# Feed-forward of a decoder kernel: quantisation over all 704 columns at once, input quantised by quarters

## The chip, the cores and the metric

The kernel runs on one core of a Trainium2 chip, as one program. The metric is the device time of one execution in microseconds (us), here the median of three runs. The core has five engines that run their own instruction streams and meet at semaphores: TensorE (PE in the profile; PEld is its weight load), VectorE (DVE), ScalarE (ACT), GpSimd (POOL) and SyncE (SP), which issues the transfers.

## The reference

Four batches of 1024 rows with 256 columns pass through two layers: a state-space scan, a cross attention and a feed-forward in the first, a cosine attention, an alignment and a mixture of experts in the second. Each adds to the residual stream x. The change lies in the first layer's feed-forward alone:

```python
BLOCK = 16
_GRID = [0.0, 0.5, 1.0, 1.5, 2.0, 3.0, 4.0, 6.0]
_MID = [0.25, 0.75, 1.25, 1.75, 2.5, 3.5, 5.0]

def fp4_quant_dequant(x):
    xb = x.reshape(shape[:-1] + (shape[-1] // BLOCK, BLOCK))
    scale = jnp.maximum(jnp.max(jnp.abs(xb), axis=-1, keepdims=True) / 6.0, 1e-12)
    xn = xb / scale
    idx = jnp.searchsorted(_MID, jnp.abs(xn))
    return (_GRID[idx] * jnp.sign(xn) * scale).reshape(shape)

def fp4_linear(x, w):
    return jnp.einsum('bsk,nk->bsn', fp4_quant_dequant(x), fp4_quant_dequant(w))

gate, y = fp4_linear(x, w_gate), fp4_linear(x, w_up)     # 256 -> 704
h = jax.nn.silu(gate) * y
out = fp4_linear(h, w_down)                              # 704 -> 256
x = x + L0_ffn(_layernorm(x))
```

So the normalised input is quantised in blocks of 16 columns, multiplied with two weight matrices of 704 columns, combined to a hidden row of 704 columns, quantised again and multiplied back to 256 columns.

## The kernel before, in words

One batch is worked off at a time, in 8 tiles of 128 rows. Each engine has its own function for the stage, with the order of its work written out by hand; semaphores carry the rest. The stage runs four times in an execution, once per batch.

`quantize` (L2177) does ten VectorE steps on a list of pieces: largest absolute value per block (L2187), scaling of it (L2189), reciprocal (L2190), scaling (L2191), multiplication of the row (L2192), two steps that find the power of two of each element (L2194, L2196), two rounding steps (L2198, L2199), and the multiplication back (L2210). For each step it goes through all pieces, and each instruction waits on VectorE's own semaphore for the step before of its own piece. With two pieces, two independent chains alternate.

`quantize_z` (L715) does this for the normalised input `z`; a piece is a pair of tiles, 512 columns. Pairs 0 and 1 are quantised one at a time within the cross attention before. Pairs 2 and 3 come together at the head of `ffn_dve` (L1000), as two pieces.

VectorE then does, for each tile k, `hidden(k)`: the product of silu(gate) and up out of PSUM (L1007), then `quantize` of the hidden row as two pieces of 352 columns (L1010), then, for the tile before the last one begun, `add`: the down result to x (L1017) with the statistics for the next normalisation. `hidden(k + 1)` stands ahead of `add(k - 1)`.

TensorE does for each tile `gate_up` (8 float32 matmuls, L938, 16 records in the trace; waits until the product of the tile before has been read), `turn` (6 transposes of the quantised hidden row, L947; waits for both pieces at L943) and `down` (6 matmuls, L956). In the loop `gate_up(k + 1)` comes first, then `turn(k)`, then `down(k - 1)`. The transposes of the input (`transpose_z`, L269) stand ahead of that loop: pair 0, gate_up(0), then pairs 1, 2 and 3 in PSUM banks 5, 6 and 7, each waiting for its pair of quantised input. `turn` uses banks 4 and 5, `down` bank 6.

ScalarE copies the transposed input to `zT` (`keep_zT`, L275), computes silu (L982) and copies the transposed hidden row (L995 to L997).

Of the kernel before, what the change touches and what calls it, by code (L numbers as in the profile page):

```python
# [29 lines left out]
FF = 704  # L30
FQ = FF // 2
FK = [(k * P, min(P, FF - k * P)) for k in range((FF + P - 1) // P)]
QB = 16
# [52 lines left out]
def program(nc, t, out):  # L86

    ctx = ExitStack()
    with ctx:
# [122 lines left out]
        def tile_stats(v, own, src, k, n, to=by_stage):  # L212

            own.wait()
            own(v.bn_stats(to.stat[:, k, :], src))
            if k >= 1:
                aggregate(v, own, k - 1, n, to)
            if k == NT - 1:
                own.wait()
                aggregate(v, own, k, n, to)  # L220
# [42 lines left out]
        def transpose_z(pe, j, wait_tile, pairs=range(NT // 2), first_bank=0):  # L263
            for g in pairs:
                for k in (2 * g, 2 * g + 1):
                    wait_tile(k)
                    for c in range(DC):
                        q = (k % 2) * DC + c
                        last = pe.transpose(psum[:, first_bank + g, q * P:(q + 1) * P], z[:, k, c * P:(c + 1) * P], ident[:, :])  # L269
                last.then_inc(zT_psum, 1)  # L270

        def keep_zT(a, j, pairs=range(NT // 2), first_bank=0):
            for g in pairs:
                a.wait_ge(zT_psum, 4 * j + g + 1)
                a.activation(zT[:, :, 2 * g * P:(2 * g + 2) * P].rearrange("p c (k x) -> p k c x", k=2),  # L275
                             psum[:, first_bank + g, :].rearrange("p (k c x) -> p k c x", k=2, c=DC),
                             ACT.Copy).then_inc(zT_ready, 1)


        r = Region(arena)  # L280
# [15 lines left out]
        r = Region(arena, scan_end)  # L296
# [400 lines left out]
        r = Region(arena, scan_end)  # L697
# [17 lines left out]
        def quantize_z(v, own, pairs):  # L715

            n = 2 * D
            quantize(v, own, [(z[:, 2 * h:2 * h + 2, :].rearrange("p k d -> p (k d)"),
                               z_scaled[:, n * h:n * (h + 1)], z_power[:, n * h:n * (h + 1)],
                               f_amax[:, n * h // QB:n * (h + 1) // QB], f_inv[:, n * h // QB:n * (h + 1) // QB])  # L720
                              for h in pairs],
                     lambda piece, last: own.bring(last, zq_ready, pairs[0] + piece + 1))
# [199 lines left out]
        r = Region(arena, scan_end)  # L922
        silu_gate = r.take(2, FF)
        hid = r.take(2, FF)
        h_scaled, h_power = r.take(FF), r.take(FF)
        hT = r.take(2, len(FK), P)
        h_amax, h_inv = r.take(2, FQ // QB), r.take(2, FQ // QB)
        assert r.at <= zq.at - 2 * NT * (D + D // QB)

        def ffn_pe(pe, own, j):  # L930

            def gate_up(k):
                if k >= 1:
                    pe.wait_ge(hid_made, k)
                for i, wT in enumerate((gateT, upT)):
                    for half in range(2):
                        for c in range(DC):
                            last = pe.matmul(psum[:, 2 * i + half, 0:FQ], zT[:, c, k * P:(k + 1) * P],  # L938
                                             wT[:, c, half * FQ:(half + 1) * FQ], start=c == 0, stop=c == DC - 1)
                last.then_inc(gu_psum, 1)  # L940

            def turn(k):
                pe.wait_ge(h_ready, 2 * (k + 1))  # L943
                if k >= 1:
                    pe.wait_ge(hT_ready, 3 * k)
                for i, (at, wide) in enumerate(FK):
                    last = pe.transpose(psum[0:wide, 4 + i // 4, (i % 4) * P:(i % 4 + 1) * P],  # L947
                                        hid[:, k % 2, at:at + wide], ident[:, :])
                last.then_inc(ht_psum, 1)

            def down(k):
                pe.wait_ge(hT_ready, 3 * (k + 1))
                if k >= 1:
                    pe.wait_ge(fres_done, k)
                for i, (_, wide) in enumerate(FK):
                    last = pe.matmul(psum[:, 6, 0:D], hT[0:wide, k % 2, i, :], downT[0:wide, i, :],  # L956
                                     start=i == 0, stop=i == len(FK) - 1)
                last.then_inc(down_psum, 1)

            pe.wait_ge(ffn_w_in, 16 * 3)  # L960
            transpose_z(pe, j, lambda k: pe.wait_ge(zq_ready, k // 2 + 1), pairs=(0,), first_bank=4)
            pe.wait_ge(zT_ready, 4 * j + 1)
            gate_up(0)
            transpose_z(pe, j, lambda k: pe.wait_ge(zq_ready, k // 2 + 1), pairs=(1, 2, 3), first_bank=4)
            for k in range(NT):
                if k + 1 < NT:
                    if k % 2:
                        pe.wait_ge(zT_ready, 4 * j + (k + 1) // 2 + 1)
                    gate_up(k + 1)
                if k == 0:  # L970
                    pe.wait_ge(zT_ready, 4 * j + 2)
                turn(k)
                if k >= 1:
                    down(k - 1)
            down(NT - 1)

        def ffn_act(a, own, j):
            def silu(k):
                a.wait_ge(gu_psum, k + 1)
                if k >= 2:  # L980
                    a.wait_ge(hid_made, k - 1)
                a.activation(silu_gate[:, k % 2, :].rearrange("p (a x) -> p a x", a=2),  # L982
                             psum[:, 0:2, 0:FQ], ACT.Silu).then_inc(sg_ready, 1)

            keep_zT(a, j, pairs=(0,), first_bank=4)
            silu(0)
            keep_zT(a, j, pairs=(1, 2, 3), first_bank=4)
            for k in range(NT):
                if k + 1 < NT:
                    silu(k + 1)  # L990
                q = k % 2
                a.wait_ge(ht_psum, k + 1)
                if k >= 2:
                    a.wait_ge(down_psum, k - 1)
                a.activation(hT[:, q, 0:4, :].rearrange("p k x -> p (k x)"), psum[:, 4, :], ACT.Copy).then_inc(hT_ready, 1)  # L995
                a.activation(hT[:, q, 4, :], psum[:, 5, 0:P], ACT.Copy).then_inc(hT_ready, 1)
                a.activation(hT[0:64, q, 5, :], psum[0:64, 5, P:2 * P], ACT.Copy).then_inc(hT_ready, 1)  # L997

        def ffn_dve(v, own, b, next_n, next_j):
            quantize_z(v, own, (2, 3))  # L1000

            def hidden(k):
                q = k % 2
                v.wait_ge(sg_ready, k + 1)
                if k >= 2:
                    v.wait_ge(ht_psum, k - 1)
                own.bring(v.tensor_tensor(hid[:, q, :].rearrange("p (a x) -> p a x", a=2),  # L1007
                                          silu_gate[:, q, :].rearrange("p (a x) -> p a x", a=2),
                                          psum[:, 2:4, 0:FQ], ALU.mult), hid_made, k + 1)
                quantize(v, own, [(hid[:, q, i * FQ:(i + 1) * FQ], h_scaled[:, i * FQ:(i + 1) * FQ],  # L1010
                                   h_power[:, i * FQ:(i + 1) * FQ], h_amax[:, i], h_inv[:, i]) for i in range(2)],
                         lambda piece, last: own.bring(last, h_ready, 2 * k + piece + 1))

            def add(k):
                v.wait_ge(down_psum, k + 1)
                xk = x_all[:, b * NT + k, :]
                own.bring(v.tensor_tensor(xk, xk, psum[:, 6, 0:D], ALU.add), fres_done, k + 1)  # L1017
                tile_stats(v, own, xk, k, next_n)

            hidden(0)  # L1020
            for k in range(NT):
                if k + 1 < NT:
                    hidden(k + 1)
                if k >= 1:
                    add(k - 1)
            norm_x(v, own, b, next_n, next_j, tiles=range(NT // 2))
            add(NT - 1)
# [6 lines left out]
        r = Region(arena, after_parts)  # L1034
# [139 lines left out]
        r = Region(arena, scan_end)  # L1174
# [37 lines left out]
        r = Region(arena)  # L1212
# [257 lines left out]
        r = Region(arena, WAVES * LW)  # L1470
# [16 lines left out]
        r = Region(arena, beside_dtw)  # L1487
# [725 lines left out]
        r = Region(arena)  # L2213
# [446 lines left out]
```

## Time and profile before

| | us |
|---|---|
| median of three runs | 3328.77 (3325.11 to 3330.94) |
| the profiled execution | 3329.13 |
| its span, first to last instruction | 3327.4 |
| TensorE busy in the span | 2758.6 (83%) |
| VectorE busy | 2433.5 (73%) |
| ScalarE busy | 1339.7 (40%) |
| GpSimd busy | 622.2 (19%) |
| mean granted TensorE clock | 0.906 of full speed |

In the chain that ended last, TensorE holds 59% and VectorE 25% of the span. The four feed-forward stages lie at about 427 to 513, 941 to 1026, 1453 to 1538 and 1931 to 2016 us. The table is an average over all stages; what a change of the feed-forward is worth is read from these four stretches. Rows of a timeline give the start, the duration, engine, line, operation, output and input, and the count of instructions that were merged; in square brackets stands the idle time of the engine just before and what ended it.

### The profile page before, as it was taken

The page shows a single profiled execution, that of the slowest core. Times are in us where ns is not written, and L with a number is a line of the kernel's source. Part 1 is how long each engine was busy: PE and PEld are TensorE (multiplying, and loading weights), DVE is VectorE, ACT ScalarE, POOL GpSimd, SP SyncE. Part 2 cuts the span into 40 slices and gives each one's busy share as a digit, 9 for nine tenths or more (in the row PEclk, how much of TensorE's full clock was granted, in tenths as well). Part 3 has the DMA queues.
Part 4 walks back from the last instruction along what each step waited for, and adds up shares of the span by engine and source line. Part 5 has one row for each costly group of instructions (what it writes and reads, how often), then busy time and mean ns, then how long its engine had stood idle before and what let it go on. Part 6 is the DMA issues. An engine that isn't in the chain of part 4 may idle for free.

```text
span 3327.4 us, 36552 instructions
## 1 busy us (share of the span) xinstructions
PE 2758.6 (83%) x12264; PEld 1576.6 (47%) x12264; DVE 2433.5 (73%) x4936; ACT 1339.7 (40%) x2455; POOL 622.2 (19%) x426
## 2 busy tenths in 40 slices
PE   4226888997889997889998888992369999999998
PEld 2003764444665344665345764441135656566564
DVE  6996687997687997678998586006877676776766
ACT  2323326773425773424773325553640131411313
POOL 2444000332100333100233000001000040310404
PEclk9557899998989998989998989996669999999999
DMA  5001000001000001000001000006020000000000
GB/s 159 0 0 45 1 1 7 23 20 53 1 1 5 22 20 57 1 1 1 23 23 46 10 0 7 23 20 127 0 34 1 1 14 1 1 14 1 14 1 13
DMA packets 57635, 65.93 MB, mean 20 GB/s; under 512 B 27757, under 2 KB 46690, under 8 KB 56802
## 3 DMA queue, kind: packets, MB, share of 16 engines
q1 hardware_dynamic: 57441, 63.51, 7.1%
q8 instruction: 103, 1.69, 0.2%
q14 instruction: 91, 0.74, 0.1%
HBM read 45.22 MB, written 9.88 MB: 17 GB/s over the span
## 4 chain that ended last, share of the span: by engine, by line
PE 59%; DVE 25%; issue 5%; ACT 4%; POOL 2%; DMA 1%; SPq 0%; DVEq 0%; ACTq 0%; POOLq 0%
PE psum L1712 14%; PE psum L383 8%; DVE arena L543 6%; PE psum L938 4%; PE psum L1772 3%; PE psum L790 3%; PE psum L1052 3%; DVE arena L538 3%; PE psum L956 3%; PE psum L770 2%; PE psum L373 2%; PE psum L374 2%; PE psum L269 2%; PE psum L781 2%; PE psum L1071 1%
## 5 line engine op out<-in xcount | busy, mean ns | idle before, releaser
L1712 PE MATMUL psum<-weights,arena 128*128 128x384 f16 x3072 | 534.9, 329 | 5.1 <-DVE arena L2068 4.0
L383 PE MATMUL psum<-arena,weights 128*128 128x512 f32 (+1 forms) x1024 | 522.6, 593 | 5.0 <-ACT arena L457 5.0
L2071 DVE SCALAR_TENSOR_TENSOR arena<-psum,arena 128x384 f32<-128x384 f32 x480 | 295.7, 616 | 193.7 <-PE psum L1712 182.6
L457 ACT ACTIVATE arena<-psum,minus_scale 128x512 f32<-128x512 f32 x512 | 350.7, 686 | 215.1 <-PE psum L383 213.3
L1712 PEld LDWEIGHTS psum<-weights,arena 128*128 128x128 f16 x3072 | 304.2, 99 | 194.3 <-issue 8.8
L598 POOL TENSOR_TENSOR arena<-arena 128x1024 f32<-128x1024 f32 x128 | 274.0, 2141 | 598.6 <-DVE arena L543 598.0
L543 DVE TENSOR_TENSOR_SCAN arena<-weights,arena 128x1026 f32<-128x1026 f32 x128 | 293.9, 2296 | 18.4 <-ACT weights L450 3.8
L246 POOL TENSOR_SCALAR shifted<-mean_var 128x4 f32<-128x4 f32 x40 | 9.8, 245 | 1287.1 <-DVE mean_var L223 1287.1
L1947 POOL TENSOR_TENSOR arena<-arena 128x512 f32<-128x512 f32 x112 | 147.6, 1321 | 509.8 <-ACT arena L1886 499.2
L383 PEld LDWEIGHTS psum<-arena,weights 128*128 128x128 f32 (+1 forms) x1024 | 166.1, 163 | 98.7 <-ACT arena L457 12.1
L450 ACT ACTIVATE weights<-arena,weights 128x512 f32<-128x512 f32 x256 | 169.1, 712 | 102.8 <-DVE arena L543 102.8
L373 PE MATMUL psum<-arena 128*128 128x512 f16 x512 | 194.5, 380 | 4.7 <-DMA arena<-arena 4.7
L374 PE MATMUL psum<-arena 128*128 128x512 f16 x512 | 194.2, 379 | 0.0
L1772 PE MATMUL psum<-weights,arena 128*128 128x512 f16 x768 | 172.5, 379 | 7.8 <-DVE x_all L2100 4.6
L938 PE MATMUL psum<-weights,z_both 128*128 128x352 f32 x512 | 171.0, 490 | 6.6 <-DVE arena L1007 3.9
L275 ACT ACTIVATE z_both<-psum 128x512 f32<-128x512 f32 x96 | 55.3, 594 | 262.1 <-PE psum L269 262.0
L551 DVE TENSOR_TENSOR arena<-arena,psum 128x1024 f32<-128x1024 f32 x128 | 156.3, 1221 | 4.4
L2100 DVE SCALAR_TENSOR_TENSOR x_all<-psum,arena,x_all 128x256 f32<-128x256 f32 x256 | 122.3, 483 | 50.0 <-PE psum L1772 44.9
L538 DVE TENSOR_TENSOR arena<-arena,psum 128x1024 f32<-128x1024 f32 x128 | 154.8, 1209 | 3.8 <-PE psum L356 3.6
L269 PE MATMUL psum<-ident,z_both 128*128 128x128 f32 x384 | 72.9, 351 | 101.7 <-DVE z_both L260 80.1
L356 PE MATMUL psum<-arena,weights 96*128 96x512 bf16 x128 | 55.8, 436 | 104.8 <-DVE arena L551 96.2
L1886 ACT ACTIVATE arena<-psum,arena 128x256 f32<-128x256 f32 x256 | 107.5, 471 | 87.5 <-PE psum L1772 87.3
(324 smaller groups left out, 4867.0 us busy)
## 6 DMA issues: line engine op xcount, KB each, us to landing
arena<-arena SPq DMA_DIRECT2D x64, 128.0 KB, 2.3
arena<-head_inv SPq DMA_DIRECT2D x32, 256.0 KB, 3.4
weights<-in_qkv SPq DMA_DIRECT2D x2, 3072.0 KB, 17.1
weights<-gate_upT_kept SPq DMA_DIRECT2D x4, 1408.0 KB, 6.4
x_all<-in_x SPq DMA_DIRECT2D x4, 1024.0 KB, 11.9
weights<-in_cWkv SPq DMA_DIRECT2D x4, 1024.0 KB, 11.3
out<-x_all SPq DMA_DIRECT2D x4, 1024.0 KB, 4.4
weights<-downT_kept SPq DMA_DIRECT2D x4, 640.0 KB, 7.0
```

Of the source, the lines that this page charges most:

```text
L373: pe.matmul(psum[:, i % 3, :], keys, q_parts[:, hd, at], start=True, stop=False)
L374: pe.matmul(psum[:, i % 3, :], keys, q_swapped_parts[:, hd % 2, at], start=False, stop=True).then_inc(s2_psum, 1)
L383: pe.matmul(psum[0:rows, 3 + turn % 2, :], value_and_ones(kt, hd), expd[:, i % 2, :], start=kt == 0, stop=kt == NT - 1).then_inc(pv2_done, 1)
L450: a.activation(dA[:, j % RING, m, 1:], dt[:, m, half * HALF:(half + 1) * HALF], ACT.Exp, scale=a_neg[:, m, s:s + 1]).then_inc(da_ready, 1)
L457: a.activation(expd[:, i % 2, :], psum[:, i % 3, :], ACT.Exp, bias=minus_scale[:, :], scale=SCALE / QK ** 2).then_inc(exp_done, 1)
L538: v.tensor_tensor(to[:, :, 1:], u[:, :, at], both(5 + 2 * j % 3), ALU.mult).then_inc(w_done, 1)
L543: v.tensor_tensor_scan(flat, dA[:, j % RING].rearrange("p m x -> p (m x)"), flat, 0.0, ALU.mult, ALU.add).then_inc(scan_done, 1)
L598: g.tensor_tensor(y[:, :, at], y[:, :, at], h[:, j % RING, :, 1:], ALU.add).then_inc(y_added, 1)
L938: last = pe.matmul(psum[:, 2 * i + half, 0:FQ], zT[:, c, k * P:(k + 1) * P], wT[:, c, half * FQ:(half + 1) * FQ], start=c == 0, stop=c == ...
L1712: last = pe.matmul(psum[:, n % PROJ_BANKS, 0:W3], zT_parts[:, of_z, c, k * P:(k + 1) * P], w_parts[:, c, e, of_w, :], start=c == 0 and j == 0,
L1772: last = pe.matmul(psum[:, O_BANKS[u % 4], :], ao_parts[:, of_a, k * P:(k + 1) * P], o_parts[:, m, of_w, :], start=j == 0, stop=j == 2)
L2071: step_ = v.scalar_tensor_tensor(qkv[:, k, :], src, router_w[:, k, e:e + 1], qkv[:, k, :], ALU.mult, ALU.add)
```

## The change

The hidden row is quantised as one piece of 704 columns instead of two of 352, in one chain of ten instructions; TensorE waits for one count per tile instead of two. Of the input, pair 2 alone is quantised at the head of the stage, and pair 3 after `hidden(1)`, ahead of `hidden(2)`. TensorE's transposes of pair 2 go to bank 7, and those of pair 3 to bank 7 as well, after `turn(1)` and `down(0)`, when the copy of pair 2 is done. ScalarE's copy of pair 3 moves to the same place in its order.

```diff
-        h_amax, h_inv = r.take(2, FQ // QB), r.take(2, FQ // QB)
+        h_amax, h_inv = r.take(FF // QB), r.take(FF // QB)
...
             def turn(k):
-                pe.wait_ge(h_ready, 2 * (k + 1))
+                pe.wait_ge(h_ready, k + 1)
...
             gate_up(0)
-            transpose_z(pe, j, lambda k: pe.wait_ge(zq_ready, k // 2 + 1), pairs=(1, 2, 3), first_bank=4)
+            transpose_z(pe, j, lambda k: pe.wait_ge(zq_ready, k // 2 + 1), pairs=(1,), first_bank=4)
+            transpose_z(pe, j, lambda k: pe.wait_ge(zq_ready, k // 2 + 1), pairs=(2,), first_bank=5)
             for k in range(NT):
...
                 turn(k)
                 if k >= 1:
                     down(k - 1)
+                if k == 1:
+                    pe.wait_ge(zT_ready, 4 * j + 3)
+                    transpose_z(pe, j, lambda t: pe.wait_ge(zq_ready, t // 2 + 1), pairs=(3,), first_bank=4)
             down(NT - 1)

         def ffn_act(a, own, j):
...
             silu(0)
-            keep_zT(a, j, pairs=(1, 2, 3), first_bank=4)
+            keep_zT(a, j, pairs=(1,), first_bank=4)
+            keep_zT(a, j, pairs=(2,), first_bank=5)
...
                 a.activation(hT[0:64, q, 5, :], psum[0:64, 5, P:2 * P], ACT.Copy).then_inc(hT_ready, 1)
+                if k == 1:
+                    keep_zT(a, j, pairs=(3,), first_bank=4)

         def ffn_dve(v, own, b, next_n, next_j):
-            quantize_z(v, own, (2, 3))
+            quantize_z(v, own, (2,))
...
-                quantize(v, own, [(hid[:, q, i * FQ:(i + 1) * FQ], h_scaled[:, i * FQ:(i + 1) * FQ],
-                                   h_power[:, i * FQ:(i + 1) * FQ], h_amax[:, i], h_inv[:, i]) for i in range(2)],
-                         lambda piece, last: own.bring(last, h_ready, 2 * k + piece + 1))
+                quantize(v, own, [(hid[:, q, :], h_scaled, h_power, h_amax, h_inv)],
+                         lambda piece, last: own.bring(last, h_ready, k + 1))
...
             for k in range(NT):
                 if k + 1 < NT:
                     hidden(k + 1)
+                if k == 0:
+                    quantize_z(v, own, (3,))
                 if k >= 1:
                     add(k - 1)
```

## Rows read from the trace of the kernel before

**Rows 1.** Stretches: busy time by engine (count), granted clock, DMA share, GB/s.

```profile
core 0: us, PE busy (x) PEld busy (x) DVE busy (x) ACT busy (x) POOL busy (x), PEclk, DMA share, GB/s
431.00:437.00 6.00, 1.25 (x7) 0.69 (x5) 6.00 (x15) 1.25 (x2) 0.00 (x0) 1.00 0.00 0
469.50:478.00 8.50, 8.50 (x38) 5.89 (x37) 8.05 (x25) 1.63 (x5) 0.00 (x0) 1.00 0.01 2
502.00:506.00 4.00, 3.35 (x11) 2.96 (x12) 1.44 (x5) 0.92 (x3) 0.00 (x0) 0.50 0.00 0
...
954.00:957.00 3.00, 3.00 (x8) 1.81 (x8) 3.00 (x13) 0.00 (x0) 0.00 (x0) 0.70 0.00 0
```

**Rows 2.** Timeline of the first feed-forward's steady part, all engines.

```profile
472.90 5.00 PE L938 MATMUL psum<-weights,z_both 128*128 128x352 f32 x16
...
477.40 0.41 DVE L1017 TENSOR_TENSOR x_all<-x_all,psum 128x256 f32 x1
...
477.74 0.82 PE L947 MATMUL psum<-ident,arena 128*128 128x128 f32 x6
...
478.73 0.89 DVE L1007 TENSOR_TENSOR arena<-arena,psum 128x704 f32<-128x704 f32 x1 [0.38 <-ACT arena L982]
...
481.27 5.00 PE L938 MATMUL psum<-weights,z_both 128*128 128x352 f32 x16
```

**Rows 3.** Timeline of VectorE: product and quantising of tile 1, two pieces.

```profile
445.39 0.89 DVE L1007 TENSOR_TENSOR arena<-arena,psum 128x704 f32<-128x704 f32 x1 [0.64 <-ACT arena L982]
446.31 0.94 DVE L2187 TENSOR_REDUCE arena<-arena 128x22 f32<-128x352 f32 x2
...
451.56 0.95 DVE L2210 TENSOR_TENSOR arena<-arena 128x352 f32<-128x352 f32 x2
452.43 0.88 DVE L1007 TENSOR_TENSOR arena<-arena,psum 128x704 f32<-128x704 f32 x1
```

**Rows 4.** Timeline of VectorE: input pair 1, one piece, in the cross attention.

```profile
413.77 0.69 DVE L2187 TENSOR_REDUCE arena<-z_both 128x32 f32<-128x512 f32 x1
414.49 0.18 DVE L2189 TENSOR_SCALAR arena<-arena 128x32 f32<-128x32 f32 x1
414.71 0.35 DVE L2190 RECIPROCAL arena<-arena 128x32 f32<-128x32 f32 x1
...
415.31 0.69 DVE L2192 TENSOR_TENSOR arena<-z_both,arena 128x512 f32<-128x512 f32 x1
416.04 0.43 DVE L2194 TENSOR_SCALAR arena<-arena 128x512 int32<-128x512 int32 x1
...
418.42 0.69 DVE L2210 TENSOR_TENSOR z_both<-arena 128x512 f32<-128x512 f32 x1
419.03 0.41 DVE L905 TENSOR_TENSOR x_all<-x_all,psum 128x256 f32 x1
```

**Rows 5.** Timeline of VectorE: input pairs 2 and 3, and what follows.

```profile
429.39 1.28 DVE L2187 TENSOR_REDUCE arena<-z_both 128x32 f32<-128x512 f32 x2
...
437.64 0.88 DVE L1007 TENSOR_TENSOR arena<-arena,psum 128x704 f32<-128x704 f32 x1
```

**Rows 6.** Groups of VectorE by line and form, 0 to 45 us (weights' quantising).

```profile
L2198 DVE SCALAR_TENSOR_TENSOR arena<-arena 128x1408 f32<-128x1408 f32 x3 | 4.7, 1610 | 0.0
...
L2194 DVE TENSOR_SCALAR arena<-arena 128x1408 int32<-128x1408 int32 x3 | 2.5, 880 | 0.0
...
L2190 DVE RECIPROCAL arena<-arena 128x88 f32<-128x88 f32 x3 | 1.8, 657 | 0.0
```

**Rows 7.** Timeline of the second feed-forward's start, all engines.

```profile
943.79 1.28 DVE L2187 TENSOR_REDUCE arena<-z_both 128x32 f32<-128x512 f32 x2
...
951.58 1.55 PE L269 MATMUL psum<-ident,z_both 128*128 128x128 f32 x8 [2.79 <-DVE z_both L2210]
...
952.98 6.39 PE L938 MATMUL psum<-weights,z_both 128*128 128x352 f32 x16
```

**Rows 8.** Timeline of TensorE: transposes of tile 7, first and second feed-forward.

```profile
502.65 1.54 PE L947 MATMUL psum<-ident,arena 128*128 128x128 f32 x6 [4.56 <-DVE arena L2210]
...
1017.46 1.54 PE L947 MATMUL psum<-ident,arena 128*128 128x128 f32 x6 [4.56 <-DVE arena L2210]
```

## The prediction, made blind

> **What bounds the kernel now.** I read the stretches of the first feed-forward first, by engine, then its timeline in order of time. Four such stages run, one per batch. The stretches show three regimes [rows 1]. At 431 to 437 us VectorE is busy without a break and TensorE for 1.25 of 6 us. At 469.5 to 478 us TensorE is busy for all 8.50 us at the full granted clock, and VectorE for 8.05. At 502 to 506 us the granted clock is 0.50, the lower of its two levels (1.2 GHz, where full is 2.4). The timeline of the middle gives the period: the gate and up matmuls of one tile start at 472.90, of the next at 481.27, so 8.37 us a tile; the product that opens VectorE's next tile (L1007) had waited 0.38 us for silu [rows 2]. So the steady part is TensorE's, with VectorE only 0.38 us a tile behind. The start is VectorE's: it quantises two input pairs for 8.25 us (429.39 to 437.64) before the product of tile 0 [rows 5]. The end is VectorE's as well: TensorE's transposes of tile 7 wait 4.56 us for the quantised hidden row [rows 8].
>
> I count time from the moment at which VectorE begins to quantise the last two input pairs (429.39 in the first stage, 943.79 in the second), and call L(k) the start of tile k's product. The mark for the end is the start of the transposes of tile 7: 502.65 - 429.39 = 73.26 us in the first stage and 1017.46 - 943.79 = 73.67 in the second [rows 5, 7, 8]. The third and fourth repeat the second.
>
> **Edit 1, 704 columns in one chain.** Before, two pieces of 352 columns alternate. Ten steps of two instructions run from 446.31 to the next instruction's start at 452.43: 6.12 us, the last result ending at 451.56 + 0.95, 6.20 us after the start [rows 3]. After, ten instructions stand in one chain, each waiting for the one before it on its own engine. The trace has such a chain, one input pair of 512 columns: each step starts 0.03 to 0.04 us after its predecessor has ended, and the whole takes 419.03 - 413.77 = 5.26 us [rows 4]. Two such pairs alternating take 8.25, so 4.13 each [rows 5]. Behind an unfinished predecessor an instruction pays a latency that the partner used to cover. That decides the sign.
>
> Sizing 704 columns: a two-operand step goes from 0.69 us at 512 columns to 1.61 at 1408, 1.03 ns a column, so 192 more columns cost 0.20 [rows 4, 6]. The reduction becomes 0.72 + 0.20 = 0.92, the multiply and the two rounding steps 0.73 + 0.20 = 0.93 each. This agrees with the only 704-column step followed by one that needs it, 445.39 to 446.31 = 0.92 [rows 3]. The two masking steps: 0.43 at 512 and 0.88 at 1408 give 0.53, with the gap 0.56 each. The reciprocal: 0.35 at 32 and 0.66 at 88 give 0.42 at 44 blocks, with the gap 0.45. The two small scalings 0.22 each. To the start of the tenth step: 0.92 + 3 x 0.93 + 2 x 0.56 + 0.45 + 2 x 0.22 = 5.72. The tenth ends 0.89 later, at 6.61, and an instruction that doesn't need it starts 0.08 before that (418.42 + 0.69 against 419.03), at 6.53. So edit 1 costs **+0.41 us a tile**, and with the product of 0.92 a tile holds VectorE for 7.45 instead of 7.04. The trace shows no chain of 704, so bounds: below, a chain without latency, 5.41 (worked out under rival 2), -0.7; above, that 5.41 times the ratio 5.26 / 4.13 of the 512-column rows, 6.89, +0.8, if the latency grew with the columns. The gap behind the 704-column step is 0.03, as at 512, so I take 0.41; of the upper side I keep +0.6 for the range, which is 0.2 x 8 x 4 = 6 us more.
>
> The Trainium skill speaks against this (VectorE: DVE Perf Modes, Rules for kernel authors): of chained VectorE operations it says to lower their count and not to mind semaphores. By it the change should gain; the 5.26 against 4.13 of the rows above speaks for the opposite, and rival 2 below prices it.
>
> That TensorE waits for one count instead of two (L943) costs nothing: it used the second piece's anyway.
>
> **Edit 2, the input by quarters.** Pair 2 alone costs 5.26 before L(0) instead of 8.25 for both [rows 4, 5]: 2.99 earlier. Pair 3 costs another 5.26, now between the hidden steps of tiles 1 and 2, and its first step waits for the end of tile 1's last (0.08 + 0.03). Together 10.52 + 0.11 for 8.25: **+2.4 us** of VectorE time. It lies where VectorE sets the pace, so nothing hides it. On TensorE's queue the transposes of pair 3 move behind the down matmuls of tile 0; what waits behind them is the gate and up matmuls of tile 3. ScalarE's copy of that pair moves likewise, ahead of the silu of tile 3. TensorE's idle time between its pieces grows there, but VectorE is later still.
>
> **The new schedule**, us from the mark. L(0) = 5.26 and L(1) = 5.26 + 7.45 = 12.71. Is TensorE in time? Gate and up of tile 1 may start when the product has left the banks, about 6.2, and silu is through 5.83 us after their start (472.90 to 478.73 [rows 2]): 12.0, so 0.7 to spare. Pair 3: 12.71 + 7.45 + 0.11 = 20.27. L(2) = 20.27 + 5.26 = 25.53. Hidden row 2 is complete at 25.53 + 0.92 + 6.61 = 33.06. Then TensorE: transposes 0.06 later, the next gate and up 3.53 after those (477.74 to 481.27), silu 5.83 after that [rows 2], so L(4) can't be before 42.48. VectorE has L(3) = 25.53 + 7.45 + 0.95 for the residual add (477.40 to 478.35) = 33.93, and would be free at 42.33. So L(4) = 42.48, and from here both engines are about equal: VectorE needs 7.45 + 0.95 = 8.40 a tile, TensorE 8.37, and the loop through both needs L(k+2) at least 7.53 + 0.06 + 3.53 + 5.83 = 16.95 after L(k). This gives L(5) = 50.88, L(6) = 59.43, L(7) = 67.83. Transposes of tile 7: 67.83 + 7.53 + 0.06 = 75.42.
>
> Against 73.26 this is +2.16 in the first stage, against 73.67 +1.75 in each of the other three: **+7.4 us**. What follows is the same work behind the same idle time (TensorE's last work before it ends at about 70.5, so 4.9 us idle instead of 4.56), so I cost the tail at nothing; its cover is that the clock falls there either way, 0.50 at 502 to 506 [rows 1]. In words: VectorE's work grows by 2.4 + 8 x 0.41 = 5.7 us a stage, and its waits in the old schedule can take in 3.5 of that, no more, because they lie in the steady part only.
>
> **Rivals.** 1. *The chain of 704 costs no more than the pair* (6.12). Then L(1) = 12.30, L(2) = 24.71, row 2 at 31.83, L(4) = 41.25, L(7) = 66.36 by TensorE's 8.37, transposes at 73.54: +0.3 and three times -0.1, so 3329 us, no change. This says that the reordering by itself gains nothing. For it: the longer a step, the smaller the share of a latency. Against: the 0.92 of the 704-column step [rows 3].
> 2. *Fewer instructions win; the side that is not slower.* The pair of 512 (8.25) and of 352 (6.12) have equal counts, so columns cost (8.25 - 6.12) / 320 = 6.66 ns and the fixed part of twenty instructions is 1.43 us [rows 3, 5]. If ten pay half of that and no latency, a tile's quantising takes 5.41. L(1) is then held by silu at 12.0, L(2) = 23.7, row 2 at 30.1, L(4) = 39.5, L(7) = 64.6, transposes at 71.1: -2.2 and three times -2.6, 10 us less, 3319. It decides from a chain price below about 5.9. Against: the chain of 512 shows the latency in nine steps of ten [rows 4]. This is the result of the Trainium skill's rule named above.
> 3. *TensorE's clock falls in the new gaps.* In the second stage the granted clock was 0.70 at 954 to 957 us, behind 2.79 us of idle time, and gate and up of tile 1 took 6.39 us against 5.00 [rows 1, 2, 7], 1.39 more. The new schedule has TensorE idle for 2.5 us ahead of pair 2's transposes in the first stage, and three times about 1.6 us by tile 3. A fall at tile 1 exceeds its 0.7 to spare by 0.7; one by tile 4 costs all of 1.39. Both in all four stages: 8.4 on top, 3345. Against: the two falls that rows show stand behind 2.79 and 4.56 us of idle time [rows 7, 8], longer than any gap of the new start.
>
> **How the numbers follow.** The profiled execution took 3329.13 us (span 3327.4), the median of the runs is 3328.77: it stands for them. 3329.13 + 7.4 = 3336.5, the forecast (+5 to +12), chance 0.55. Rival 1 (-2 to +5) 0.24, rival 3 (over +12) 0.12, rival 2 0.09. The range 3328 to 3344 leaves out rival 2 and the upper end of rival 3. 0.2% is 6.7 us, about what a measurement of this kernel can tell from no change. The forecast lies just beyond it: of its 0.55 some 0.41 are above 6.7. Slower 0.41 + 0.12 = 0.53; same 0.14 + 0.24 = 0.38; faster 0.09.
>
> **What would show it.** In the profile after: the chain of 704 from its reduction to the next product at 6.5 us (6.1 would be rival 1, 5.4 rival 2); L(0) 5.3 us behind the mark; TensorE idle at pair 3's transposes; L1007's wait for silu gone from 0.38 to almost nothing in tiles 5 to 7; transposes of tile 7 at 75.4. A granted clock below full between tiles 1 and 4 would be rival 3. The forecast is wrong if the steps of the chain start with no gap behind their predecessors.

## The result, and the profile after

The changed kernel takes 3336.87 us (median of 11 executions, 3335.22 to 3339.72), the kernel before 3328.13 in the same rounds (11 executions): ratio 1.0028, 95% interval 1.0019 to 1.0036. It is slower by 8.7 us, where 7.4 were forecast (3336.5 us). The profiled execution took 3339.72 us, the longest of the eleven and 10.6 more than that of before (3329.13). The four feed-forward stages, from the mark to the start of the last residual add, account for 10.5 of them: 341.6 us after, 331.1 before, in sum.

The stretches of the first stage, moved so that they lie at the same distance from the mark as in [rows 1] (the mark is now 429.79; the tail is cut at the transposes of tile 7):

```profile
core 0: us, PE busy (x) PEld busy (x) DVE busy (x) ACT busy (x) POOL busy (x), PEclk, DMA share, GB/s
431.40:437.40 6.00, 3.31 (x16) 2.09 (x15) 5.72 (x10) 1.84 (x3) 0.00 (x0) 1.00 0.00 0
469.90:478.40 8.50, 8.50 (x36) 5.88 (x35) 7.76 (x15) 1.57 (x4) 0.00 (x0) 1.00 0.01 2
443.50:447.00 3.50, 3.50 (x8) 2.08 (x8) 3.29 (x7) 0.92 (x3) 0.00 (x0) 0.61 0.00 0
505.00:509.00 4.00, 3.65 (x12) 3.17 (x13) 1.13 (x4) 0.92 (x3) 0.00 (x0) 0.50 0.00 0
```

The start looks better: TensorE is busy for 3.31 of 6 us where it was 1.25. The middle is as full as before. The third line is new: a stretch at a lower granted clock, 0.61, by tile 2. The trace of before has its fall one tile earlier, by tile 1 (0.72 at 437 to 443 us, then 1.00 at 443 to 449), where the changed kernel has none. VectorE's count of instructions in the middle falls from 25 to 15. Its busy time falls too, from 8.05 to 7.76 us, although one wait of about 0.38 us lies in both stretches: the gaps between the steps of a lone chain are not counted as busy.

Those gaps are seen in the timeline of VectorE: the first and the last step of the new chain in tile 0, then the whole chain of tile 1 and the head of pair 3 behind it. They answer to [rows 3, 4]:

```profile
435.98 0.89 DVE L2195 TENSOR_REDUCE arena<-arena 128x44 f32<-128x704 f32 x1
...
441.71 0.89 DVE L2218 TENSOR_TENSOR arena<-arena 128x704 f32<-128x704 f32 x1
442.51 0.88 DVE L1014 TENSOR_TENSOR arena<-arena,psum 128x704 f32<-128x704 f32 x1
443.43 0.89 DVE L2195 TENSOR_REDUCE arena<-arena 128x44 f32<-128x704 f32 x1
444.35 0.19 DVE L2197 TENSOR_SCALAR arena<-arena 128x44 f32<-128x44 f32 x1
444.57 0.43 DVE L2198 RECIPROCAL arena<-arena 128x44 f32<-128x44 f32 x1
445.03 0.19 DVE L2199 TENSOR_SCALAR arena<-arena 128x44 f32<-128x44 f32 x1
445.25 0.89 DVE L2200 TENSOR_TENSOR arena<-arena 128x704 f32<-128x704 f32 x1
446.18 0.53 DVE L2202 TENSOR_SCALAR arena<-arena 128x704 int32<-128x704 int32 x1
446.74 0.53 DVE L2204 TENSOR_SCALAR arena<-arena 128x704 f32<-128x704 f32 x1
447.30 0.89 DVE L2206 SCALAR_TENSOR_TENSOR arena<-arena 128x704 f32<-128x704 f32 x1
448.23 0.89 DVE L2207 SCALAR_TENSOR_TENSOR arena<-arena 128x704 f32<-128x704 f32 x1
449.16 0.89 DVE L2218 TENSOR_TENSOR arena<-arena 128x704 f32<-128x704 f32 x1
450.08 0.69 DVE L2195 TENSOR_REDUCE arena<-z_both 128x32 f32<-128x512 f32 x1
```

In tile 1, every step that needs the one before it starts 0.03 to 0.04 us behind that one's end. In tile 0 the same chain runs from 435.98 to the next product at 442.51, 6.53 us; the two alternating pieces took 6.12 [rows 3]. Pair 3 follows (450.08) and takes 5.27 us to the product of tile 2 at 455.35.

TensorE, and what waits for it, around the moved transposes and in the steady part (timeline of all engines, answering to [rows 2]), and the tail (answering to [rows 8]):

```profile
455.58 0.63 PE L269 MATMUL psum<-ident,z_both 128*128 128x128 f32 x4 [1.82 <-DVE z_both L2218]
...
456.29 5.00 PE L938 MATMUL psum<-weights,z_both 128*128 128x352 f32 x16
...
472.36 0.89 DVE L1014 TENSOR_TENSOR arena<-arena,psum 128x704 f32<-128x704 f32 x1 [0.37 <-ACT arena L986]
...
480.73 0.89 DVE L1014 TENSOR_TENSOR arena<-arena,psum 128x704 f32<-128x704 f32 x1
...
489.38 0.89 DVE L1014 TENSOR_TENSOR arena<-arena,psum 128x704 f32<-128x704 f32 x1 [0.23 <-ACT arena L986]
...
497.75 0.89 DVE L1014 TENSOR_TENSOR arena<-arena,psum 128x704 f32<-128x704 f32 x1
...
505.35 1.54 PE L947 MATMUL psum<-ident,arena 128*128 128x128 f32 x6 [4.72 <-DVE arena L2218]
```

TensorE waits 1.82 us for pair 3, and gate and up of tile 3 stand behind that. VectorE's wait for silu, 0.38 us a tile before, is 0.37 at tile 4, nothing at 5 and 7 and 0.23 at 6: VectorE's slack is nearly used up. The transposes of tile 7 start at 505.35, 75.56 us behind the mark; before it was 73.26 [rows 5, 8].

The starts of the products, L(0) to L(7), and of the transposes of tile 7, in us behind the mark, with the kernels of the next section. Each row is one of the four stages of a profiled execution; before and the changed kernel are shown with two.

| kernel, stage | L0 | L1 | L2 | L3 | L4 | L5 | L6 | L7 | transposes of 7 |
|---|---|---|---|---|---|---|---|---|---|
| before, first | 8.25 | 16.00 | 23.04 | 32.60 | 40.97 | 49.34 | 57.71 | 66.09 | 73.26 |
| before, second | 8.26 | 16.41 | 23.45 | 33.00 | 41.38 | 49.75 | 58.12 | 66.49 | 73.67 |
| forecast | 5.26 | 12.71 | 25.53 | 33.93 | 42.48 | 50.88 | 59.43 | 67.83 | 75.42 |
| changed, first | 5.27 | 12.72 | 25.56 | 33.80 | 42.57 | 50.94 | 59.59 | 67.96 | 75.56 |
| changed, second | 5.76 | 13.22 | 26.06 | 34.30 | 43.07 | 51.44 | 60.08 | 68.46 | 76.05 |
| chain only, first | 8.25 | 16.38 | 23.83 | 33.39 | 41.76 | 50.40 | 58.77 | 67.41 | 75.01 |
| quarters only, first | 5.37 | 12.41 | 24.81 | 33.19 | 41.56 | 49.93 | 58.30 | 66.68 | 73.85 |
| pair 3 beside row 1, second | 5.39 | 12.85 | 23.29 | 34.00 | 42.38 | 51.01 | 59.39 | 68.03 | 75.62 |
| pair 3 beside row 2, first | 5.77 | 12.82 | 19.84 | 31.59 | 40.14 | 48.90 | 57.27 | 65.65 | 72.82 |
| pair 3 spread, first | 5.38 | 12.41 | 19.44 | 29.47 | 39.56 | 48.42 | 56.79 | 65.17 | 72.34 |

### The profile page after: what moved, and what is told of

The parts are those of the page before. It is cut to its first block, busy times and chain, and to the rows that moved or that the text cites. A ratio compares the mean times of both kernels' runs of the same rounds, so it can differ in the third digit from the quotient of the medians.

```text
span 3338.0 us, 36236 instructions
## 1 busy us (share of the span) xinstructions
PE 2762.2 (83%) x12264; PEld 1577.1 (47%) x12264; DVE 2443.6 (73%) x4616; ACT 1340.0 (40%) x2455; POOL 621.8 (19%) x426
## 4 chain that ended last, share of the span: by engine, by line
PE 50%; DVE 33%; issue 6%; ACT 4%; POOL 2%; DMA 1%; SPq 0%; DVEq 0%; ACTq 0%; POOLq 0%
PE psum L1720 13%; DVE arena L543 8%; PE psum L383 5%; DVE arena L538 4%; PE psum L790 3%; PE psum L1780 3%; PE psum L1060 3%; PE psum L770 3%; PE psum L938 2%; PE psum L781 2%; PE psum L956 2%; PE psum L269 1%; DVE arena L551 1%; DVE z_both L1448 1%; PE psum L323 1%
```

## Experiments

The theory: a VectorE instruction that waits for the one just before it starts only behind that one's end, and a second chain in alternation covers this; the change removes the partner, and puts pair 3 where VectorE sets the pace. The rivals: that the count of instructions or their width sets the price, and that one of the two edits carries the loss alone.

**Each edit alone.** First the chain of 704, with the input as before:

```diff
...
-                quantize(v, own, [(hid[:, q, i * FQ:(i + 1) * FQ], h_scaled[:, i * FQ:(i + 1) * FQ],
-                                   h_power[:, i * FQ:(i + 1) * FQ], h_amax[:, i], h_inv[:, i]) for i in range(2)],
-                         lambda piece, last: own.bring(last, h_ready, 2 * k + piece + 1))
+                quantize(v, own, [(hid[:, q, :], h_scaled, h_power, h_amax, h_inv)],
+                         lambda piece, last: own.bring(last, h_ready, k + 1))
```

> The hidden row as one chain of 704 columns, the input as before (pairs 2 and 3 together at the head). Theory (an unfinished predecessor costs a latency that a second chain covers): a tile's quantising takes 6.53 us to the next instruction instead of 6.12; tile 1's product still waits for silu (16.0 and 16.4 us behind the mark), so the loss counts from tile 1 on only; transposes of tile 7 at 74.5 us in the first stage and 74.9 in the others, +1.2 us a stage, 5 us in all: 3333 to 3334 us, ratio 1.0015. Rival (fewer instructions win): 5.4 us a tile, TensorE's 8.37 us a tile decides, no later than before, ratio 1.000 or below.

Measured: 3334.01 us, ratio 1.0017 (1.0008 to 1.0026). Transposes of tile 7 at 75.01, 75.02, 75.34 and 74.70 us in the four stages, 5.9 us later than before in sum (5 expected). The chain alone makes the kernel slower: ten instructions fewer a tile did not make up for the lost partner. Its product of tile 1 still waits 0.59 us for silu, so part of tile 0's longer chain is hidden there.

Then the quarters, with two pieces of 352 kept:

```diff
-            quantize_z(v, own, (2, 3))
+            quantize_z(v, own, (2,))
...
                     hidden(k + 1)
+                if k == 0:
+                    quantize_z(v, own, (3,))
```

(with TensorE's and ScalarE's order as in the change)

> The input by quarters as in the change, the hidden row in two pieces of 352 as before. Theory: the reordering by itself gains nothing, since pair 3's chain of 512 columns (5.3 us) stands on VectorE's path between tiles 1 and 2: product of tile 0 at 5.3 us behind the mark, of tile 1 at 12.3, of tile 2 at 24.7, transposes of tile 7 at 73.5 (before: 73.3 and 73.7), so 3328 to 3331 us, ratio 1.000. Rival (the quarters bring what they are named for, and the loss of the change is the chain's alone): 3.0 us a stage earlier, ratio 0.9965. Rival (the quarters carry the whole loss): as the change, ratio 1.0028.

Measured: 3328.07 us, ratio 1.0001 (0.9992 to 1.0010). The timeline of VectorE in the first stage (mark 426.71) shows where the 3 us go that the start wins:

```profile
439.12 0.87 DVE L1014 TENSOR_TENSOR arena<-arena,psum 128x704 f32<-128x704 f32 x1
...
446.26 0.69 DVE L2196 TENSOR_REDUCE arena<-z_both 128x32 f32<-128x512 f32 x1
...
450.92 0.69 DVE L2219 TENSOR_TENSOR z_both<-arena 128x512 f32<-128x512 f32 x1
451.52 0.88 DVE L1014 TENSOR_TENSOR arena<-arena,psum 128x704 f32<-128x704 f32 x1
...
459.90 0.89 DVE L1014 TENSOR_TENSOR arena<-arena,psum 128x704 f32<-128x704 f32 x1 [0.47 <-ACT arena L986]
```

Tile 1 starts at 12.41 instead of 16.00, tile 2, behind pair 3 (446.26 to 451.52), at 24.81 instead of 23.04. VectorE's wait ahead of tile 3, 1.66 us before, is 0.47. From tile 4 on the spacing is 8.37 us as before, and the end comes at 73.85. The reordering by itself gains and loses nothing that can be measured, and both rivals for this run fall, since 0.9965 and 1.0028 lie outside the interval.

**The price of a lone chain, by itself.** The kernel before with the two pieces one after the other, so that instructions, widths and count stay:

```diff
-                quantize(v, own, [(hid[:, q, i * FQ:(i + 1) * FQ], h_scaled[:, i * FQ:(i + 1) * FQ],
-                                   h_power[:, i * FQ:(i + 1) * FQ], h_amax[:, i], h_inv[:, i]) for i in range(2)],
-                         lambda piece, last: own.bring(last, h_ready, 2 * k + piece + 1))
+                for i in range(2):
+                    quantize(v, own, [(hid[:, q, i * FQ:(i + 1) * FQ], h_scaled[:, i * FQ:(i + 1) * FQ],
+                                       h_power[:, i * FQ:(i + 1) * FQ], h_amax[:, i], h_inv[:, i])],
+                             lambda piece, last: own.bring(last, h_ready, 2 * k + i + 1))
```

> The kernel before with the two pieces of 352 columns quantised one after the other, not in alternation: same twenty instructions of the same widths a tile, another order. Theory: both are chains without a partner, 4.2 to 4.3 us each, so 8.5 us a tile in place of 6.1; VectorE needs 10.3 us a tile and becomes the bound of the steady part; transposes of tile 7 at about 88 us, +14.5 us a stage, 3385 us. Rival (the count of instructions or their width sets the price): 6.1 us a tile, 3328 us.

Measured: 3382.06 us (one execution). The timeline of VectorE, first piece of tile 0 and the next starts:

```profile
436.17 0.52 DVE L2188 TENSOR_REDUCE arena<-arena 128x22 f32<-128x352 f32 x1
436.72 0.18 DVE L2190 TENSOR_SCALAR arena<-arena 128x22 f32<-128x22 f32 x1
436.93 0.29 DVE L2191 RECIPROCAL arena<-arena 128x22 f32<-128x22 f32 x1
...
438.79 0.53 DVE L2199 SCALAR_TENSOR_TENSOR arena<-arena 128x352 f32<-128x352 f32 x1
439.35 0.53 DVE L2200 SCALAR_TENSOR_TENSOR arena<-arena 128x352 f32<-128x352 f32 x1
...
440.46 0.52 DVE L2188 TENSOR_REDUCE arena<-arena 128x22 f32<-128x352 f32 x1
...
444.65 0.88 DVE L1007 TENSOR_TENSOR arena<-arena,psum 128x704 f32<-128x704 f32 x1
```

And two rounding steps of tile 0 in the kernel before, in alternation:

```profile
442.06 0.95 DVE L2198 SCALAR_TENSOR_TENSOR arena<-arena 128x352 f32<-128x352 f32 x2
442.93 0.95 DVE L2199 SCALAR_TENSOR_TENSOR arena<-arena 128x352 f32<-128x352 f32 x2
```

The same twenty instructions take 444.65 - 436.17 = 8.48 us where they took 6.12 in alternation. A rounding step of 352 columns repeats after 0.56 us (438.79 to 439.35); two of them in alternation passed in 0.87 (442.06 to 442.93). Neither count nor width changed, so the order alone costs 2.36 us a tile. The transposes of tile 7 moved to 87.67 us, 88 expected.

**The other direction, more instructions.** Four pieces of 176 columns in the kernel before:

```diff
...
-                pe.wait_ge(h_ready, 2 * (k + 1))
+                pe.wait_ge(h_ready, 4 * (k + 1))
...
+                w = FF // 4
+                quantize(v, own, [(hid[:, q, i * w:(i + 1) * w], h_scaled[:, i * w:(i + 1) * w],
+                                   h_power[:, i * w:(i + 1) * w], h_amax[:, i], h_inv[:, i]) for i in range(4)],
+                         lambda piece, last: own.bring(last, h_ready, 4 * k + piece + 1))
```

> The kernel before with the hidden row in four pieces of 176 columns: forty instructions a tile. Theory: the fixed part of an instruction is there too, 0.07 us when others alternate with it (1.43 us for twenty), so a tile's quantising takes 7.5 us, VectorE needs 9.4 us a tile and becomes the bound of the steady part; transposes of tile 7 at about 81 us, +7.5 us a stage, 3359 us. If only a chain's latency cost anything and not the count, 6.1 us a tile and 3329 us.

Measured: 3346.92 us (one execution), a tile's quantising 7.21 us (435.34 to 442.55), the steady period 8.97. Count does cost, but less than I had expected: 1.09 us for twenty more instructions, 0.055 each, not 0.07. The transposes of tile 7 came at 79.9 and 78.6 us, 4.9 to 6.6 later than before, where 7.5 were expected, and the total stayed 12 us below the expected 3359. The kernel's two pieces are the best of one, two and four.

**A partner for the new chain.** In the changed kernel, pair 3 beside hidden row 1 instead of behind it:

```diff
-                quantize(v, own, [(hid[:, q, :], h_scaled, h_power, h_amax, h_inv)],
-                         lambda piece, last: own.bring(last, h_ready, k + 1))
+                pieces = [(hid[:, q, :], h_scaled, h_power, h_amax, h_inv)]
+                n = 2 * D
+                if k == 1:
+                    pieces.append((z[:, 6:8, :].rearrange("p k d -> p (k d)"), z_scaled[:, 3 * n:4 * n],
+                                   z_power[:, 3 * n:4 * n], f_amax[:, 3 * n // QB:4 * n // QB],
+                                   f_inv[:, 3 * n // QB:4 * n // QB]))
+                quantize(v, own, pieces, lambda piece, last: own.bring(last, h_ready, k + 1)
+                         if piece < 1 else own.bring(last, zq_ready, 4))
...
-                if k == 0:
-                    quantize_z(v, own, (3,))
```

> The changed kernel with one edit: pair 3 is quantised as a second chain beside the 704-column chain of hidden row 1, in place of behind it. Same columns, same instructions. Theory (an unfinished predecessor costs, a partner covers it): both together take 9.5 us (1216 columns at 6.66 ns and 1.43 us of fixed part) in place of 6.5 + 5.4 = 11.9, so the product of tile 2 moves from 25.6 to 23.2 us behind the mark. Row 1 is ready later, and TensorE then holds tile 3 at 32.8 and tile 4 at 41.2 (change: 33.8 to 34.3 and 42.6 to 43.1), transposes of tile 7 at 74.3 (change: 75.6 to 76.1): 1.3 us a stage less than the change, 3331 to 3332 us, ratio 1.0010. Rival (704 columns in one instruction are slow in themselves): 11.9 us stay, ratio 1.0026.

Measured: 3336.12 us, ratio 1.0027 (1.0016 to 1.0039): no gain over the change, where 1.0010 was expected. The price is as the theory has it; the timeline of the first stage (mark 428.42) shows both that and where it was lost:

```profile
442.28 0.89 DVE L2199 TENSOR_REDUCE arena<-arena 128x44 f32<-128x704 f32 x1
...
451.35 1.54 PE L947 MATMUL psum<-ident,arena 128*128 128x128 f32 x6 [3.98 <-DVE arena L2222]
451.82 0.88 DVE L1014 TENSOR_TENSOR arena<-arena,psum 128x704 f32<-128x704 f32 x1
452.69 3.75 PE L956 MATMUL psum<-weights,arena 128*128 128x256 f32 x12
...
462.59 0.89 DVE L1014 TENSOR_TENSOR arena<-arena,psum 128x704 f32<-128x704 f32 x1 [2.45 <-ACT arena L986]
```

Row 1 and pair 3 together take 451.82 - 442.28 = 9.54 us (expected 9.5; in the change 6.53 + 5.4), and tile 2 starts at 23.3 to 23.7 us instead of 25.6 to 26.1. But row 1 is ready only with the last step of both. TensorE idles 3.98 us for it; its transposes and the down matmuls behind them then take 1.54 and 3.75 us instead of 0.87 and 2.95, and a stretch of this run puts the granted clock there at 0.62:

```profile
451.30:455.30 4.00, 3.95 (x15) 3.50 (x16) 3.83 (x7) 0.92 (x3) 0.00 (x0) 0.62 0.00 0
```

Gate and up of tile 3 are late, and VectorE waits 2.45 us for silu. So the saving of 2.4 us turned into a wait. My expectation for the total had left out that the clock would fall in that gap: tile 3 came at 34.0 to 34.6 us instead of 32.8. In the first stage the transposes and down matmuls account for 1.47 us of that.

**A version without the two costs.** Two pieces of 352, pair 2 alone at the head, and pair 3 as a third chain beside hidden row 2, its transposes behind the down matmuls of tile 2 (the second cut is against the changed kernel):

```diff
...
+                if k == 2:
+                    pieces.append((z[:, 6:8, :].rearrange("p k d -> p (k d)"), z_scaled[:, 3 * n:4 * n],
+                                   z_power[:, 3 * n:4 * n], f_amax[:, 3 * n // QB:4 * n // QB],
+                                   f_inv[:, 3 * n // QB:4 * n // QB]))
...
-                if k == 1:
+                if k == 3:
                     pe.wait_ge(zT_ready, 4 * j + 3)
```

> Two pieces of 352; pair 2 alone at the head; pair 3 as a third chain beside the two of hidden row 2, its transposes behind the down matmuls of tile 2. Theory: with partners the 512 columns cost 4.1 us instead of the 5.4 that the change pays for them, and they lie where VectorE would wait for TensorE (1.66 us ahead of tile 3): hidden row 2 with pair 3 takes 10.3 us, product of tile 3 at 31 to 32 us behind the mark, of tile 4 at 39.8 to 40.5 (before 41.0 and 41.4), transposes of tile 7 1 us earlier than before in each stage: 3324 to 3326 us, ratio 0.9987. Rival (partners cover nothing): 5.3 us for pair 3, ratio 1.000 or above.

Measured: 3323.56 us, ratio 0.9989 (0.9980 to 0.9998), the fastest of all. Timeline of VectorE in the first stage (mark 427.04), from the three chains of row 2 on:

```profile
447.80 0.95 DVE L2200 TENSOR_REDUCE arena<-arena 128x22 f32<-128x352 f32 x2
448.66 0.68 DVE L2200 TENSOR_REDUCE arena<-z_both 128x32 f32<-128x512 f32 x1
...
457.84 0.41 DVE L1030 TENSOR_TENSOR x_all<-x_all,psum 128x256 f32 x1
...
458.63 0.87 DVE L1014 TENSOR_TENSOR arena<-arena,psum 128x704 f32<-128x704 f32 x1
```

The three chains take 10.04 us, so pair 3 costs 3.92 beside its partners instead of 5.4, and the product of tile 3 starts without a wait, at 31.59 (before 32.60). The transposes of tile 7 come 0.44, 1.25, 0.84 and 1.22 us earlier than before in the four stages, 3.8 in sum. The medians differ by 3.8 us as well, but that is luck: up to the last add the four stages of the profiled execution are only 2.3 us shorter (table of the next section). The interval just excludes no change.

The same with tile 6 beside row 2 and tile 7 beside row 3:

```diff
...
+                n, t = D, k + 4
+                if k in (2, 3):
+                    pieces.append((z[:, t, :], z_scaled[:, t * n:(t + 1) * n], z_power[:, t * n:(t + 1) * n],
+                                   f_amax[:, t * n // QB:(t + 1) * n // QB], f_inv[:, t * n // QB:(t + 1) * n // QB]))
```

> As the run with pair 3 beside hidden row 2, but its tile 6 (256 columns) beside row 2 and its tile 7 beside row 3. Theory: each adds 2.1 us to a row in place of 4.1 to one, TensorE is starved less; product of tile 3 at 30 us behind the mark, of tile 4 at 39, of tile 5 at 48.4 (there 48.5 to 48.9), transposes of tile 7 at 72.0 to 72.4 (there 72.4 to 72.8): 3322 to 3324 us, ratio 0.9985, not to be told from that run. Rival (it costs TensorE more, since two rows are late): ratio 1.000.

Measured: 3325.39 us, ratio 0.9994 (0.9985 to 1.0003). The transposes of tile 7 are 0.5 us earlier than in the run before in the first stage and 0.6 in sum over the four; the totals can't tell the two apart, and this one's interval includes no change. The total lies above the 3322 to 3324 us expected.

## Why the prediction was right

**The chain's price** was right to the hundredth: 6.53 us to the next instruction, 6.61 forecast and 6.62 measured (435.98 to 441.71 + 0.89) to the end. It came from a lone chain in the trace of before, that of an input pair of 512 columns, and two slopes. The run with the pieces in sequence shows the cause by itself: the same instructions, 2.36 us dearer for want of a partner. Rival 1 (6.12) falls with the 6.53, and rival 2, fewer instructions, with that and the chain alone (1.0017). Fewer instructions do help where nothing else changes: of lone chains, twenty instructions took 8.48 us and ten for the same columns 6.53; of alternating ones, forty took 7.21 and twenty 6.12. What the edit did was to halve the count and take the partner away, and that costs 0.41 us a tile. The Trainium skill says of chained VectorE operations to lower their count and not to mind semaphores (VectorE: DVE Perf Modes, Rules for kernel authors). For this edit the measurement (ratio 1.0017 for the chain alone) decides against it.

**The quarters** cost and won what was worked out: 5.27 us for each lone pair, tile 0 at 5.27. That they gain nothing (rival 1's remark) is shown by the run with them alone.

**The schedule** was met within 0.16 us at each of the eight products of the first stage. The sum, +7.4 us, was a little small; that the time itself came within 0.4 us is in part luck, since it was added to 3329.13, which lies 1.0 above the median of before in these rounds. Up to the transposes of tile 7 the four stages came out at +2.30, +2.39, +2.41 and +2.03, 9.1 in sum. The term that was too small is L(0): I set it to 5.26 in all four, but in the second and third the product had to wait for silu (0.41 and 0.42 us), since gate and up of tile 0 ran there in part at the lower clock and took 7.5 us against 5.00 (timeline of the second stage, mark 946.94):

```profile
944.36 7.51 PE L938 MATMUL psum<-weights,z_both 128*128 128x352 f32 x16 [0.69 <-ACT z_both L275]
...
952.70 0.89 DVE L1014 TENSOR_TENSOR arena<-arena,psum 128x704 f32<-128x704 f32 x1 [0.41 <-ACT arena L986]
```

The trace of before has 7.14 us there in its second stage; I used the rows of its tile 1 [rows 7] and left tile 0 out. With that time product 0 would have come at about 5.39, as in the fourth stage (7.13 us there), so this row gives only 0.13 of the 0.5 us. Before, product 0 came at 8.25 in any case: by starting 3 us earlier the change laid open a delay that the second pair used to cover. Together L(0) makes up 1.2 of the 1.7 us by which the 9.1 exceed the sum; the rest is about 0.14 a stage.

**The tail** I had costed at nothing. From the transposes of tile 7 to the start of the last add it took 10.22, 8.88, 8.88 and 8.86 us before and 9.17, 9.76, 9.76 and 9.56 after: -1.05 and three times about +0.8, 1.4 in sum. The idle time ahead of it was about the same (4.56 and 4.72). All of the difference lies in the down matmuls of tile 6, shown for the first stage, before and after, and then for the second, before and after:

```profile
503.98 5.22 PE L956 MATMUL psum<-weights,arena 128*128 128x256 f32 x12
506.68 4.17 PE L956 MATMUL psum<-weights,arena 128*128 128x256 f32 x12
...
1018.79 3.88 PE L956 MATMUL psum<-weights,arena 128*128 128x256 f32 x12
1024.33 4.76 PE L956 MATMUL psum<-weights,arena 128*128 128x256 f32 x12
```

What differs is how long the clock stays low behind the transposes: in the second stage the granted clock at 1020 to 1023 us was 0.89 before, and 0.59 in the same stretch behind the transposes after (1025.53 to 1028.53). The forecast's cover for this term, that the clock falls there either way, held; that it then stays low equally long did not. Why the length differs is not shown. 9.1 + 1.4 is the 10.5 us of the profiled executions. The medians differ by 8.7; a single execution of one kernel lies up to 7 us from its median, so the last 2 us stay open.

The other kernels' tails moved as well. Against before, in us, summed over the four stages of the profiled execution; the last column is the difference of the medians, each against before in its own rounds:

| kernel | transposes of 7 | tail | up to the last add | medians |
|---|---|---|---|---|
| changed | +9.1 | +1.4 | +10.5 | +8.7 |
| chain only | +5.9 | +2.6 | +8.5 | +6.6 |
| quarters only | +1.2 | -1.8 | -0.6 | +0.7 |
| pair 3 beside row 1 | +9.0 | +1.7 | +10.7 | +9.4 |
| pair 3 beside row 2 | -3.8 | +1.5 | -2.3 | -3.8 |
| pair 3 spread | -4.3 | +1.3 | -3.0 | -1.3 |

So a stage's gain up to the transposes of tile 7 is not yet the kernel's: here the four tails gave back up to 1.8 us or took up to 2.6. And the whole of a single profiled execution says little about a stage: that of the chain alone was only 1.4 us longer than that of before, with its four stages 8.5 longer.

**Rival 3**, the clock in the new gaps, did happen, and cost nothing there. In the first and the second stage:

```profile
443.54 6.67 PE L938 MATMUL psum<-weights,z_both 128*128 128x352 f32 x16
...
974.00 6.32 PE L938 MATMUL psum<-weights,z_both 128*128 128x352 f32 x16
```

Gate and up of tile 2 took 6.67 us in the first stage (0.61 in the stretches above) and those of tile 3 took 6.32 in the second (granted clock 0.54 at 974 to 977 us) and 6.34 in the third, where 5.00 is the time at full clock. These times ended while VectorE was still busy: products 2 and 3 started without a wait in all stages. The forecast's reason against it, that falls stand behind longer gaps only, was wrong: the gaps ahead of the first fall were 2.55 us, at tile 1, and 1.75 us just before it, and those ahead of the second 1.59 and 1.82. The run with the partner shows the case where such a fall does reach the path; in the run with the quarters alone gate and up of tile 3 took 6.61 us, and the product of tile 3 waits 0.47 us for silu behind them.

**The edits add to more than their sum** in the profiled executions: 5.9 us for the chain alone and 1.2 for the quarters alone, up to the transposes of tile 7, against 9.1 together. Of the 2.0 us between, about 0.7 is tile 0's wait for silu, which the quarters alone show less of (product 0 at 5.36 to 5.39 us in all four stages). The rest fits the waits, though no run tests it by itself: in the run with the chain alone VectorE still waits for silu at tiles 1 and 3 (0.59 and 1.23 us in the first stage), which hides part of the longer chains; the quarters remove these waits, and then every 0.41 us counts. The medians (6.6 and 0.7 against 8.7) can't show it: each ratio's interval is about 3 us wide to either side.

## What to carry to other kernels

Before two short chains on one engine are merged into a wide one, look in the trace for a lone chain: its start-to-start spacing against that of two alternating ones gives the price, which the number of instructions saved does not tell by itself. Work that is moved out of the start of a stage is won only if it lands where its engine waits; here VectorE waited ahead of tiles 1, 3 and later, and not ahead of tile 2, where pair 3 was put. A piece that must be done anyway is the cheapest partner for a chain, but the row that it accompanies becomes late, and someone may be waiting for that row.

## What the runs showed of the hardware

The tail behind the same idle time of 4.6 to 4.7 us took from 8.9 to 10.2 us, because the down matmuls of tile 6 took between 3.9 and 5.2 us, with the clock at its lower level for different lengths. Between the profiled executions of before and after this moved a stage by up to 1 us either way, with no change in the work of the tail. And a granted clock below full stood in the changed kernel behind gaps of 2.55 and 1.75 us (tile 2, first stage) and of 1.59 and 1.82 us (tile 3, second stage), where the rows of before had shown falls behind 2.79 and 4.56.

On VectorE, a step that needs the one just before it started 0.03 to 0.04 us behind that one's end; two steps of 352 columns that don't need each other, 0.53 us each when alone, passed together in 0.87.
